# An attention block with compressive memory: all value products in three f16 parts, row normalisations on ScalarE, and a new order of each step

## What is computed

```python
def attention(x):                      # x: (8, 512, 256), after a layer normalisation of its rows
    H, DK, DV, LSEG = (16, 64, 64, 128)
    # q, k, v = x @ Wq, x @ Wk, x @ Wv; four segments of 128 rows, scanned in order
    def step(carry, seg):
        M, Z = carry                   # a 64x64 memory and a 64-vector for each sequence and head
        scores = einsum('bhid,bhjd->bhij', q, k) * scale, masked above the diagonal
        att_dot = softmax(scores) @ v
        sq, sk = elu(q) + 1, elu(k) + 1
        att_mem = sq @ M / (sq @ Z.T)
        M_new, Z_new = M + sk.T @ v, Z + sk.sum(rows)
        out = (gate * att_mem + (1 - gate) * att_dot) @ Wo
x = x + layernorm(attention(layernorm(x)))
x = x + layernorm(ffn(layernorm(x)))   # ffn: three cycles of a small gated net
```

## Time and profile before

| | us |
|---|---|
| median of 3 runs | 1027.13 (1026.92 to 1029.09) |
| the profiled execution | 1026.99 |
| its span, first to last instruction | 1025.2 |

### The profile page before, as it was taken

How to read it: one execution, slowest core, us unless ns; L and a number is a source line. 1 busy time by engine, 2 the same in 40 slices (tenths; PEclk the granted TensorE clock), 3 DMA queues, 4 the chain that set the end, 5 groups by cost and what they waited for, 6 DMA issues and landing times.

```text
span 1025.2 us, 21046 instructions
## 1 busy us (share of the span) xinstructions
PE 958.7 (94%) x8004; PEld 677.2 (66%) x8004; DVE 825.9 (81%) x1464; ACT 654.1 (64%) x1428; POOL 614.8 (60%) x752
## 2 busy tenths in 40 slices
PE   5899999999999999999999999999999889999971
PEld 2577777777777777777777776777777755333430
DVE  5879798978888888879897978797979564588785
ACT  5757575658575755576666556757575554777872
POOL 3466767546666764476767635767676362456563
PEclk9999999999999999999999999999999899999995
DMA  7000000000000000000000000000000002200025
GB/s 195 33 21 2 22 2 21 2 22 1 22 2 22 2 22 1 21 2 22 2 22 1 22 1 22 2 22 2 12 2 29 7 12 80 94 1 0 1 49 116
DMA packets 17042, 23.97 MB, mean 23 GB/s; under 512 B 7472, under 2 KB 9264, under 8 KB 16432
## 3 DMA queue, kind: packets, MB, share of 16 engines
q1 hardware_dynamic: 15472, 18.58, 6.6%
q10 hardware_dynamic: 1472, 4.06, 1.2%
HBM read 13.97 MB, written 8.65 MB: 22 GB/s over the span
## 4 chain that ended last, share of the span: by engine, by line
PE 88%; DVE 5%; ACT 3%; issue 2%; POOL 1%; POOLq 0%; DVEq 0%
PE ps L1302 24%; PE ps L1424 11%; PE ps L1319 7%; PE ps L1381 6%; PE ps L1356 6%; PE ps L1366 5%; PE ps L1346 5%; PE ps L1569 4%; PE ps L1582 4%; PE ps L1396 3%; PE ps L1409 3%; PE ps L1564 3%; PE ps L1379 2%; PE ps L1334 2%; PE ps L1277 1%
## 5 line engine op out<-in xcount | busy, mean ns | idle before, releaser
L1302 PE MATMUL ps<-arena 128*128 128x512 f16 x1152 | 274.4, 383 | 5.5 <-DVE arena L938 3.1
L682 ACT ACTIVATE arena<-ps,arena 128x128 f32<-128x128 f32 x512 | 141.9, 375 | 116.6 <-DVE arena L985 116.6
L1302 PEld LDWEIGHTS ps<-arena 128*128 128x128 f16 x1152 | 109.7, 98 | 119.2 <-DVE arena L961 6.0
L961 DVE STREAM_TRANSPOSE arena<-ps 128x1024 f32<-128x1024 f32 x96 | 145.2, 1513 | 3.5 <-PE ps L1302 3.4
L1424 PE MATMUL ps<-arena 128*128 128x256 f32 x544 | 120.3, 380 | 0.0
L1424 PEld LDWEIGHTS ps<-arena 128*128 128x128 f32 x544 | 102.2, 190 | 13.8 <-ACT arena L702 0.8
L489 POOL TENSOR_TENSOR arena<-arena 128x260 f16<-128x260 f32 x64 | 42.7, 666 | 113.1 <-ACT arena L697 113.1
L478 POOL TENSOR_TENSOR arena<-arena 128x256 f32<-128x256 f32 x128 | 93.2, 728 | 19.4 <-DVE arena L1001 19.4
L482 POOL TENSOR_TENSOR arena<-arena 128x256 f32<-128x256 f32 x128 | 94.6, 739 | 10.0
L689 ACT ACTIVATE arena<-ps 128x512 f16<-128x512 f32 (+1 forms) x128 | 77.0, 602 | 36.2 <-PE ps L1356 36.0
L480 POOL TENSOR_TENSOR arena<-arena 128x256 f32<-128x256 f32 x128 | 93.3, 729 | 10.0
(11 more groups left out here) (125 smaller groups left out, 1996.4 us busy)
## 6 DMA issues: line engine op xcount, KB each, us to landing
x_rows<-arena SPq DMA_DIRECT2D x17, 256.0 KB, 2.0
arena<-x_rows SPq DMA_DIRECT2D x4, 1024.0 KB, 8.6
arena<-in_L_attn_x_dram SPq DMA_DIRECT2D x124, 32.0 KB, 1.7
out_dram<-arena SPq DMA_DIRECT2D x18, 128.0 KB, 3.0
arena<-in_L_attn_Wq_dram ACTq DMA_DIRECT2D x2, 512.0 KB, 4.7
arena<-in_L_attn_Wk_dram ACTq DMA_DIRECT2D x2, 512.0 KB, 6.3
arena<-in_L_attn_Wv_dram ACTq DMA_DIRECT2D x2, 512.0 KB, 7.8
arena<-in_L_attn_Wo_dram SPq DMA_DIRECT2D x8, 128.0 KB, 4.4
```

Of the source, the lines that this page charges most:

```text
L682: last = act.activation(Pr[:, par, j, :], s_bank[:, par, j * P:(j + 1) * P], ACT.Exp, bias=negm[:, par, j:j + 1])
L961: dve.transpose(dst[:, d0:d0 + 32], bank.rearrange("p w (d c) -> p d w c", c=C)).then_inc(x_free, 1)
L1302: last = pe.matmul(bank[:, w, :], xc[:, lx, k, w * P:(w + 1) * P], W16[lw][:, k, i, :], start=(n == 0), stop=(n == 5))
```

## The change

1. All value products are three f16 products. `PT32` is gone; `PT16` holds high and low part for both parities, `vsplit` holds all of v. Each f32 product (two instructions) becomes three f16 ones. ACT's `v_high` and POOL's `v_low` handle 520 columns instead of 260, and DVE's `low_p` runs for both parities.
2. `n_norm`, `y_norm` and `x2_norm` move from DVE to ACT, as a scale and a bias for each row. POOL makes the bias as well: `shift` has four instructions for the two of `deviation`. y is read by `y_stats` and `y_norm` straight from its PSUM bank, and the copy `take_y` is gone in the steps (not in the last one after them).
3. `scores` and `values` wait for the second `low_p` alone.
4. `project_out` is issued in two halves of eight matmuls, and the order of the step is another on PE, DVE, ACT and POOL. N's bank comes after K3 instead of after K2.

```diff
-STEP_JOBS = ["Q1", "K1", "A0", "A1", "A2", "A3", "Q2", "Y", "K2", "N", "Q3", "K3", "F", "Q0", "K0"]
+STEP_JOBS = ["Q1", "K1", "A0", "A1", "A2", "A3", "Q2", "Y", "K2", "Q3", "K3", "N", "F", "Q0", "K0"]
...
-                    hi, lo = (v[:, g, :, 0:DV1] for v in vsplit)
+                    hi, lo = (v[:, g, :, :, 0:DV1] for v in vsplit)
                     pool.tensor_tensor(lo, v_units(s, g), hi, ALU.subtract).then_inc(vl_done, 1)
 
+                def shift(rs, nb, mv, stat, done, part, n, k):
+
+                    pool.wait_ge(stat, n * 4)
+                    pool.tensor_tensor(rs, mv[:, :, 1], eps, ALU.add).then_inc(part, 1)
+                    pool.tensor_tensor(nb, mv[:, :, 0], minus, ALU.mult).then_inc(part, 1)
+                    pool.wait_ge(part, 3 * k + 1)
+                    pool.tensor_tensor(rs, rs, mhalf, ALU.pow).then_inc(part, 1)
+                    pool.wait_ge(part, 3 * k + 3)
+                    pool.tensor_tensor(nb, nb, rs, ALU.mult).then_inc(done, 2)
...
-                    dst = PT16[:, 0] if par == 0 else PT32
                     act.wait_ge(pt_full, bp * 32 + 8 * s + 2 * g + par + 1)
-                    act.activation(dst.rearrange("p j i -> p (j i)"), s_bank[:, par, :],
+                    act.activation(PT16[:, par, 0].rearrange("p j i -> p (j i)"), s_bank[:, par, :],
                                    ACT.Copy).then_inc(p_copied, 1)
...
+                def rescale(dst, src, nb, rs):
+
+                    for w in range(2):
+                        last = act.activation(dst[:, w * D:(w + 1) * D], src[:, w * D:(w + 1) * D], ACT.Identity,
+                                              scale=rs[:, w:w + 1], bias=nb[:, w:w + 1])
+                    return last
+
+                def y_norm(bp, s):
+
+                    b, n = t_job(bp, s, "Y")
+                    act.wait_ge(y_rstd, 2 * (bp * NSEG + s + 1))
+                    rescale(row, t_bank[b], r_nb, r_rs).then_inc(t_free[b], 1)
...
-                def low_p(bp, s, g):
+                def low_p(bp, s, g, par):
                     G = bp * 16 + 4 * s + g
-                    hi, lo = (PT16[:, n].rearrange("p j i -> p (j i)") for n in range(2))
-                    dve.wait_ge(p_copied, 2 * G + 1)
-                    dve.tensor_tensor(lo, s_bank[:, 0, :], hi, ALU.subtract).then_inc(p_low, 1)
+                    hi, lo = (PT16[:, par, n].rearrange("p j i -> p (j i)") for n in range(2))
+                    dve.wait_ge(p_copied, 2 * G + par + 1)
+                    dve.tensor_tensor(lo, s_bank[:, par, :], hi, ALU.subtract).then_inc(p_low, 1)
...
                     if bp * 16 + G > 0:
-                        pe.wait_ge(p_copied, 2 * (bp * 16 + G))
-                        pe.wait_ge(p_low, bp * 16 + G)
+                        pe.wait_ge(p_low, 2 * (bp * 16 + G))
...
-                    for a in range(2):
-                        j = 2 * half + a
+                    for u in range(4):
+                        j, par = 2 * half + u // 2, u % 2
                         for i, (lp, lv) in enumerate(((0, 0), (0, 1), (1, 0))):
-                            pe.matmul(pm_bank[:, 0, 2 * a * DV1:(2 * a + 1) * DV1], PT16[:, lp, j, :],
-                                      vsplit[lv][:, g, j, 0:DV1], start=(i == 0), stop=(i == 2))
-                        last = pe.matmul(pm_bank[:, 0, (2 * a + 1) * DV1:(2 * a + 2) * DV1], PT32[:, j, :],
-                                         v[:, GP * (g % 2) + j, 1, 0:DV1], start=True, stop=True)
+                            last = pe.matmul(pm_bank[:, 0, u * DV1:(u + 1) * DV1], PT16[:, par, lp, j, :],
+                                             vsplit[lv][:, g, par, j, 0:DV1], start=(i == 0), stop=(i == 2))
```

More of the change, by code:

```diff
@@ L1072, in step @@
                     to_rows(bp * 32 + 8 * s + 8, (0,))
+                    to_rows(bp * 32 + 8 * s + 8, (1,))
+                    take_q(bp, s, 1)
                     take_k(bp, s, 1)
-                    to_rows(bp * 32 + 8 * s + 8, (1,))
+                    low_p(bp, s, 0, 0)
+                    low_p(bp, s, 0, 1)
                     divide(bp, s, 0, 0)
                     maxima(bp, s, 1, 0)
-                    if ahead:
-                        n_stats((s + 2) % 4, 128 * (bp + 1 + (s + 2) // 4), m + 3)
+                    divide(bp, s, 0, 1)
@@ L1101, in step @@
[L1101 to L1103 removed]
+                    low_p(bp, s, 2, 0)
+                    low_p(bp, s, 2, 1)
                     take_k(bp, s, 3)
@@ L1115, in step @@
                         take_k(bp, s, 0)
-                    divide(bp, s, 3, 0)
-                    if not last:
                         take_x(bp, s, 5)
```

213 lines of the change are left out of this document (119 added, 94 removed).

## The result

| | before | after |
|---|---|---|
| median of the runs, us | 1027.8 (1026.92 to 1029.09) | 1018.62 (1014.84 to 1018.93) |
| ratio, 95% interval | | 0.9901 [0.9875, 0.9928] |
| the profiled execution, us | 1026.99 | 1018.6 |
| its span, us; clock | 1025.2; 0.982 | 1016.8; 0.978 |
| mean interval from one output projection to the next, the first 15, us | 50.36 | 49.72 |

The kernel is 0.9% faster (1018.62 against 1027.8 us). The direction and the range (987 to 1019) held, but the gain is 8.4 us in the profiled execution where 21 were forecast. The time lies where rival 2 put it (1015 to 1025), not in the forecast's own 997 to 1015. The same kernel in a later comparison gave 1019.33 (1018.47 to 1022.22), ratio 0.9918 [0.9899, 0.9938].

A forecast was written before the change was run, and what follows sets the result against it. The prediction took PE's instructions to bound the steps, with DVE full where two steps meet. 1026.99 us less 41.0 of PE work, plus 23.2 of waits there, less 3.2 elsewhere: 1006.0 us, range 987 to 1019.

The forecast's parts named there:

- rival 2: More waits, still faster: half way to the 2.6 us bound between steps and +0.2 a step, 1015 to 1025 us; chance 0.12.
- the wait at values 3,0: Late in each step, PE ahead of values 3,0: a wait of about 0.15 us in the new order.
- the seam's 1.55 us: Between two steps, values 3,0 to values 0,0: DVE's list needs 15.15 us, PE 13.6, so PE waits 1.55, 15 times.
- the three seams of fourth segments: Step changes after a fourth segment: divide 3,1 0.9 us shorter, remember missing on PE; counted with the same wait as others.
- the last step: Last of 16 steps: f16 products save 2.56 us of PE work there, as in each step.
- PE's work: 256 f32 products become f16 triples: 0.16 us saved each, 2.56 us a step, 41.0 us in all.
- Rival 4: Value products on PE: f16 bound by weight loads, three take 0.29 us, slower, 1053 us; chance 0.08 together with rival 3.
- Work moved between engines: Per step: DVE falls from 44.0 to 41.9 us, ACT comes to some 37, POOL to 39 to 42; extra costs nothing.
- the second chain: Between two steps, through ACT's v_high, exp_q 1 and exponentials to PE's A2: ends at 15.0 us, nearly with DVE's list.
- The rest of the step: Outside the step change: scores 3 loses a 0.53 us wait, 0.3 us of new waits come; about -0.2 a step, -3 us.
- Rival 1: Between two steps: no new wait, DVE's mean room suffices; 983 to 996 us, chance 0.27.
- rival 3: Score buffer released later, PE's filler runs out for each group: about 3.3 us a step, 1060 us; chance 0.08 with Rival 4.

The follow-up runs named there:

- the kernel with both edits: Kernel after, with ACT's v_high 1 behind group 0's exponentials, and n_stats, n_shift, n_norm just ahead of y_stats, y_shift, y_norm: 1008.41 us.
- the filled kernel: The kernel with all three edits, plus idle PE matmuls ahead of values 1,0, 2,0, 3,0 and turn_probs 2 in the last step: 1002.9 us.
- the kernel with all three edits: The kernel with both edits, plus DVE's split of N ahead of divide 2,0 and ACT's take_n ahead of exp_k 3: 1006.62 us, run again 1004.58 us.

## Why the prediction was right in kind and wrong in size

The sum was -41.0 + 23.2 - 3.2 = -21.0 us, and the profiled execution gave -8.4. By intervals: the first 15 were forecast at -18.2 and gave -9.6 (8.5 short), the last at -2.8 and gave +2.0 (4.8 short), and 0.8 us more than forecast were won ahead of and behind them. The steps that failed are four: the wait at values 3,0, which cancelled the gain of 0.2 a step; the seam's 1.55 us, measured at 1.87; the three seams of fourth segments, counted as the others; and the last step, taken as one of sixteen.

**PE's work: right.** -2.71 us a step of pieces' own times, forecast 2.56. Twelve f16 products take 0.36 us in the chain (the last row of the kernel with both edits, 539.74), so three take 0.09. By the rule in the Trainium skill (TensorE: Matmul & The Clock Gate, LDWEIGHTS) twelve loads of 128 columns are an estimated 1.28 us; the trace doesn't agree with it for these f16 loads, each of which lasts 98 ns while the matmuls start 30 ns apart. Rival 4 falls with the 0.36 us.

**Work moved between engines: right.** DVE 42.40 us (41.9), ACT 36.48 (37), POOL 37.66, below the 39 to 42. v_high of 520 columns follows another after 0.55 us, as taken. v_low took 1135 ns, inside its bounds, and nobody waited for it. The rows of n_stats (537.01) were there without a wait, as taken from the earlier trace rows.

**The seam: right in kind, 0.3 too small.** Forecast 1.55 us of waits; in the 11 regular intervals they are 1.70, 1.96 or 1.98, mean 1.87. The place, both chains and DVE's 14.95 us were as worked out. The term that was mis-sized is the second chain: "together 14.6, and A2 must wait for the copy of A0 (some 0.4 us): 15.0" measured 15.36. Up to the end of the exponentials it took 9.61 us (529.43 to 539.04, forecast 9.8); from the last turn_probs to the end of A2 it took 5.70 (539.09 to 544.79), where 4.8 and 0.4 were put down. That is the seam shown, with 1.70 us of waits, as in four of the 11. The other seven have 1.96 or 1.98, and a term that the sum lacked: DVE's addition of 128x4 ahead of divide 3,0, which takes 0.48 us behind POOL instead of 0.17 and lets divide 3,0 start late. That it is worth this is seen in the filled kernel: with 0.16 us for it the first interval is as long as the second (48.88 and 48.87), with 0.75 it is 49.44.

**The rest of the step: a step that failed.** "about 0.15 us at scores 3 and 0.15 us at values 3,0" made a gain of 0.2 a step. The wait of scores 3 went, as forecast, but values 3,0 has 0.57 + 0.22 = 0.79 us, so nothing was won. The list there was walked: maxima, split, take_x 4, divide 2,1 and two low_p take 6.8 us (522.06 to 528.83), against some 6.3 us of PE's own. A difference of two sums of more than 6 us was stated to a tenth, and its working isn't in the prediction.

Together these two are 0.5 us a regular interval; PE's work won 0.15 more than said, and -0.84 was measured for -1.21. That is 4 us of the 8.5.

**"I count these three seams as the others": wrong.** At the fourth segments PE has no remember while DVE's list is nearly as long. There the interval was 49.24 us before and after: waits rose from 1.85 to 3.86 (scores 3 0.77, scores 0 0.57, and the seam 1.9 and more). 1.2 us each, 3.6 in all. The fifteenth interval gives the other 0.8; it has 10.2 us at half clock where the kernel before has 6.8, and how much of the 0.8 that is isn't shown.

**The last step was taken as one of sixteen: wrong.** It has no projection to cover, so `low_p` of both parities holds PE three times for 1.13 us (values 1,0, 2,0, 3,0), and at turn_probs 2 it waits 0.87 and 0.54. Before, it waited 1.98 and 1.17 at two values, 0.64 at a scores and 0.54 at a turn_probs. Then the stretch at half clock came. The kernel after, 826.00 to 833.00 in the columns of the earlier trace rows:

```profile
826.00:833.00 7.00, 7.00 (x26) 3.87 (x25) 4.95 (x10) 1.42 (x3) 4.30 (x6) 0.51 0.00 0
```

The clock there is 0.51, that is 1.2 GHz. From recall 3,1 to the net's second product it takes 11.17 us (825.58 to 836.75); in the kernel with all three edits, run again, with full clock there, 8.41 (814.65 to 823.06). The stretch costs 2.8 us. The kernel with both edits, without it, has 41.87 us, 0.74 less than before: 2.0 of the 4.8 are waits and work, 2.8 the clock. The two rows:

```profile
825.58 0.80 PE L1425 MATMUL ps<-arena 128*128 128x130 f32 x4 [1.10 <-DVE arena L1058]
...
836.75 3.60 PE L1638 MATMUL ps<-arena 128*128 128x512 f32 x8
```

**The rivals.** Rival 1 (steps near 48, no new wait) and rival 3 (waits at scores 1 to 3) are not what the trace shows; in the regular step no scores waits. Rival 2 is, in part: the seam is beyond its forecast and the rest won nothing. But these two make only 4 of the 12.6 us that were missing. The rest of rival 2's hit is luck: the fourth segments, the last step and its 2.8 us at half clock stood in no rival. Its 12% were too few even so: my 1.55 was what two lists need if every piece follows the last one at once, and stood as a middle.

## What to carry to other kernels

Where several lists end at one place within some tenths of a microsecond, what is saved on the bounding engine can be worth about half (here 1.4 of 2.5 us a step), and what is taken from one list almost nothing: here -0.02 and -0.16 us a regular step apart, -0.56 together. A wait worked out as the difference of two lists came out too low here, at the seam (1.55 for 1.87) and at values 3,0 (0.15 for 0.79), and every place where an engine's work leaves out a piece (a last segment, a last step) wants a sum of its own. A cheaper operation that another part must prepare (here the low part) has to be tried with the order that brings that part early: alone, it made this kernel 7% slower. And a mean over all steps hides both a stretch at half clock and a collision of two short instructions: compare like intervals one by one.

## What the runs showed of the hardware

An addition of 128x4 on VectorE (`seq_sums`) took 0.16 or 0.17 us when nothing ran on GpSimd beside it, in all steps of the kernel before. In the first 15 intervals of the kernels of the new order it started 0.008 to 0.5 us behind the start of a 128x256 f32 instruction on GpSimd, took 0.2 to 0.75 us, and ended within 0.05 us of that instruction's end; in three places where the two started within 0.005 us of each other it took 0.16 or 0.17. So in these traces it is held until GpSimd's instruction is done; how that comes about they don't show. A regular interval is up to 0.55 us longer by it.

The granted clock of TensorE fell to half in stretches: in the old order with f16 products in nearly every step, shortly behind a wait of 2.6 us; in the 15th interval of every kernel of the new order and of the kernel before (797.7 to 804.6), in or behind a wait of 2.41 to 3.36 us, for 3.4, 6.8 or 10.2 us; and behind waits of 0.97, 0.97, 0.96 and 1.10 us in the last step in some runs of a kernel and not in others of the same kernel. What makes it come in one run and not in the next, or last longer in one, stays open. Two profiles of the same kernel can differ by 2.8 us by this alone, a third of the gain that was to be explained.
